# GpSimd's wait for a landing, ahead of every second head group instead of every one

## The chip, the cores and the metric

One core of one Trainium2 chip runs the whole program. The metric is the time of one execution on the device, in microseconds; a kernel's time is the median of its runs.

## What is computed

The input is a batch of two images of 64 x 64 pixels with 256 channels, float32. Three layers follow one another.

1. A deformable attention. `x` is group-normalized, multiplied by `qkv_w` and convolved depthwise (3 x 3). From the queries come, for each pixel, each of 8 head groups and each of 9 points, an offset and a mask. At each of these 72 places the keys and values of the group's 32 channels are read, bilinearly, from the four pixels around it:

```python
v00 = gather(y0i, x0i)
v01 = gather(y0i, x1i)
v10 = gather(y1i, x0i)
v11 = gather(y1i, x1i)
out = v00 * (1 - wx) * (1 - wy) + v01 * wx * (1 - wy) + v10 * (1 - wx) * wy + v11 * wx * wy
...
attn = jnp.einsum('bgpc,bgpkc->bgpk', qh, k)
attn = jax.nn.softmax(attn, axis=-1)
out = jnp.einsum('bgpk,bgpkc->bgpc', attn, v)
```

   A projection and a residual end the layer.
2. A dense attention over the 4096 pixels of an image, with 8 heads of 32, whose Q, K, V and output projections are convolutions of width 3, after a layer norm.
3. A mixture of 8 experts (256 to 1024 to 256) with a capacity, each pixel going to its best expert.

## The kernel before

**The table and the gathers.** The kernel first makes the convolved maps of image 0 (`stage_maps`) and then a table in DRAM (`stage_tables`): one row of 256 floats (1 KB) for each pixel and head group, which holds the keys and values of the four pixels around a place. A record (`sa_rec`) has, for each tile of 128 pixels, the row numbers and the weights. The work of layer 1 behind the table is the class `Sampling` (line 559). It goes over 64 tiles of 128 pixels (32 for each image); a tile has 8 head groups. For one head group of one tile, `gather` (line 655) has GpSimd issue nine indirect DMAs (line 664), one for each point, each of 128 rows of 1 KB (one row to each partition, 131,072 bytes). Together they fill one slot, `sa_slot`, of 1152 keys and as many values a partition. There are eight slots, one for each head group; so there are 512 trains of nine, 4608 gathers in all.

Ahead of a train GpSimd waits for up to three things: at head group 0 for the tile's record (`tile_in`); from tile 1 on for the slot to be free, that is for `values_made` of the same head group of the tile before; and for the landing of the train before it (`gathered` of the head group before).

**Who uses the slots.** VectorE waits for `gathered[g]` by itself, in `q_times_k` (line 710), multiplies the keys with the query, and sums in `scores` (line 716). After four head groups come `logits`, an exponential on ScalarE (line 788) and `weights`; `values` (line 762) then multiplies the values of each of the four slots by the weights, and that is what frees a slot. TensorE sums the products (line 819) and projects.

**How it is laid beside other work.** The sampling is cut into 30 pieces a tile, and VectorE, ScalarE, TensorE and SyncE do them in program order between the steps of other stages; `turn` gives each engine the pieces up to a target. GpSimd has nothing else to do in these stages: `pool` (line 670) issues, at the start of a stage, all trains that the stage's own pieces make possible, one after the other. Every stage ends with a barrier of all engines. The stages that the sampling runs beside are, by their stretches in the profile: the maps of image 1 (`stage_maps_ahead`, 517 to 1700 us); the projections and the attention of the first query block of image 0 (to 1857 and 2057); the tables of image 1 (`stage_tables_ahead`, to 2723); then projections and attention in turn: 2723 to 2880 and to 3492, to 3855 and 4905, to 5077 and 6554 (image 0), to 6684 and 6931, to 7059 and 7729, to 7857 and 8803 (image 1). A projection stage can begin only when the sampled tiles that it reads are stored. The last gather is issued at 8416 us. After 8803 come the last projection, the last attention without sampling (8892 to 9949), mixing and routing (`stage_mix_route`, which scatters rows to the experts with indirect DMAs at line 2166), and the experts.

**The dense attention's loop.** In `stage_attention` a slot is one block of 128 keys against 1024 queries. 38 slots (`TILE_SLOTS`) take one tile of sampling along. In each slot VectorE does one `a_above` (line 1654) of a bank that TensorE fills (`a_late`, line 1506), and TensorE waits for VectorE to free that one bank.

Of the kernel before, what the change touches and what calls it, by code (L numbers as in the profile page):

```python
# [17 lines left out]
G, K, HC = 8, 9, C // 8  # L18
# [540 lines left out]
class Sampling:  # L559
# [95 lines left out]
    def gather(self, pool, n, g):  # L655
        if g == 0:
            pool.wait_ge(self.tile_in[n % 2], 32 * (n // 2) + 32)
        if n > 0:
            pool.wait_ge(self.values_made, G * (n - 1) + g + 1)
        if G * n + g > 0:  # L660
            before = G * n + g - 1
            pool.wait_ge(self.gathered[before % G], 16 * K * (before // G + 1))
        for k in range(K):
            pool.indirect_dma_start(  # L664
                out=self.slot[g][:, k, :, :, :].rearrange("p c a n -> p (c a n)"), out_offset=None,
                in_=self.s["table"][n // TILES].rearrange("t p (g n) -> (t p g) n", g=G),
                in_offset=bass.IndirectOffsetOnAxis(ap=self.rec[n % 2][:, g * K + k:g * K + k + 1].bitcast(U32), axis=0),
            ).then_inc(self.gathered[g], 16)
# [2091 lines left out]
```

## Time and profile before

| | us |
|---|---|
| Median of 3 runs (10973.56 to 10993.63) | 10989.29 |
| The profiled execution | 10980.76 |
| Its span, first to last instruction | 10979.0 |
| Busy in the span: TensorE / VectorE / ScalarE / GpSimd | 7942.1 / 5184.5 / 3774.6 / 5030.1 |

The profiled execution is 8.5 us under the median, and 1.8 us of it lie outside the span. A gather's duration is the time in which GpSimd makes the descriptors of one indirect DMA; the transfer itself runs on the DMA engines behind it. "Issue" as what ended a wait means that the engine waited for nothing that the profile shows.

### The profile page before, as it was taken

What the parts mean: (1) busy time and instruction counts of PE and PEld (TensorE: products, weight loads), DVE (VectorE), ACT (ScalarE), POOL (GpSimd) and SP (SyncE); (2) the same over time, 40 slices, a digit from 0 to 9 for tenths busy, and PEclk for the clock granted to TensorE, in tenths of its full rate; (3) what the DMA queues carried; (4) which work ended last, traced back from release to release, by engine and by line L of the source; (5) the groups of instructions that cost most, each with busy time, mean ns of one, the idle gap of its engine ahead of it and who ended that gap; (6) DMA issues with size and microseconds to landing.
All of it is one profiled execution on the core that took longest, in us unless ns stands there. A gap on an engine that the chain in (4) does not pass through costs nothing. (4 is left out here: it accounts for less than half of the span.)

```text
span 10979.0 us, 96354 instructions
## 1 busy us (share of the span) xinstructions
PE 7942.1 (72%) x31522; PEld 4244.0 (39%) x31522; DVE 5184.5 (47%) x10029; ACT 3774.6 (34%) x5495; POOL 5030.1 (46%) x4864
## 2 busy tenths in 40 slices
PE   7635554642686378876888867688588979998699
PEld 3623222442343144333443433343344434444366
DVE  7432323544454355554655545455454346663233
ACT  2100001300253045442555543255255625552132
POOL 1065655555566656665665666566564000000322
PEclk9867776875898689887998888798799979998799
DMA  3824334565443344434434334443443121104221
GB/s 122 315 83 114 102 100 142 174 205 164 144 126 94 124 126 123 117 111 135 123 116 124 109 114 141 148 127 103 146 118 92 34 83 47 54 19 131 95 78 53
DMA packets 658544, 1283.57 MB, mean 117 GB/s; under 512 B 189043, under 2 KB 398218, under 8 KB 643408
## 3 DMA queue, kind: packets, MB, share of 16 engines
q0 software_dynamic: 234240, 639.57, 19.2%
q1 hardware_dynamic: 405392, 562.58, 17.2%
q10 hardware_dynamic: 18432, 75.51, 1.7%
q8 instruction: 243, 3.98, 0.2%
q14 instruction: 237, 1.94, 0.1%
HBM read 1003.44 MB, written 278.91 MB: 117 GB/s over the span
## 5 line engine op out<-in xcount | busy, mean ns | idle before, releaser
L664 POOL DMA_INDIRECT sa_slot<-s_table,sa_rec x4608 | 4773.1, 1036 | 3610.2 <-DMA sa_slot<-s_table,sa_rec 1554.8
L1654 DVE CUSTOM_DVE_ANT_0 a_above<-a_late,a_above 128x512 f32<-128x512 f32 x1600 | 1102.7, 689 | 1696.8 <-PE a_late L1506 1030.3
L1561 PE MATMUL a_ctx<-a_p,a_v 128*64 128x512 f32 x6400 | 1669.8, 645 | 102.6 <-issue 101.6
L1595 ACT ACTIVATE a_above<-a_diff 128x512 f32<-128x512 f32 x1600 | 956.5, 598 | 2270.6 <-PE a_diff L1494 1268.8
L1586 ACT ACTIVATE a_p<-a_s 128x1024 f32<-128x1024 f32 x1600 | 1629.2, 1021 | 179.8 <-PE a_s L1544 123.2
L710 DVE TENSOR_TENSOR sa_slot<-sa_slot,sa_q 128x1152 f32<-128x1152 f32 x512 | 694.1, 1356 | 1728.3 <-DMA sa_slot<-s_table,sa_rec 1710.6
L1506 PE MATMUL a_late<-a_k,a_q 96*128 96x512 f32 x1600 | 831.4, 520 | 426.0 <-DVE a_pair_max L1654 355.3
L819 PE MATMUL sa_sums<-keep_ident,sa_vals 128*128 128x128 f32 x4608 | 688.6, 299 | 589.0 <-DVE sa_vals L762 586.7
L1494 PE MATMUL a_diff<-a_kd,a_q 96*128 96x512 f32 x1600 | 745.9, 466 | 506.7 <-DMA a_q<-s_q 434.6
L1544 PE MATMUL a_s<-a_q,a_k 98*128 98x512 f32 x3200 | 1079.5, 422 | 30.8 <-ACT a_p L1586 30.6
L819 PEld LDWEIGHTS sa_sums<-keep_ident,sa_vals 128*128 128x128 f32 x4608 | 616.4, 157 | 686.3 <-DVE sa_vals L762 606.9
L1506 PEld LDWEIGHTS a_late<-a_k,a_q 96*128 96x128 f32 x1600 | 324.1, 203 | 1344.8 <-issue 824.3
L1561 PEld LDWEIGHTS a_ctx<-a_p,a_v 128*64 128x64 f32 x6400 | 422.1, 144 | 904.7 <-issue 818.2
L2161 POOL MEMSET x_ctx<- 128x2 f32 x2 | 0.2, 104 | 1532.6 <-POOLq L75 1532.6
L1982 DVE TENSOR_REDUCE a_chunk_max<-a_max 128x1 f32<-128x512 f32 x896 | 553.1, 681 | 309.2 <-PE a_max L1858 309.1
L716 DVE TENSOR_REDUCE sa_dots<-sa_slot 128x36 f32<-128x1152 f32 x512 | 691.0, 1350 | 7.0
L762 DVE TENSOR_TENSOR sa_vals<-sa_slot,sa_corner 128x1152 f32<-128x1152 f32 x512 | 681.4, 1355 | 1.8
L1544 PEld LDWEIGHTS a_s<-a_q,a_k 98*128 98x128 f32 x3200 | 602.8, 199 | 161.5 <-ACT a_p L1586 44.8
L1933 ACT ACTIVATE a_p<-a_s 128x1024 f32<-128x1024 f32 x448 | 455.0, 1024 | 452.6 <-PE a_s L1891 447.3
L1494 PEld LDWEIGHTS a_diff<-a_kd,a_q 96*128 96x128 f32 x1600 | 331.3, 207 | 642.5 <-DMA a_q<-s_q 437.0
L1160 PE MATMUL p_c<-p_hT,p_w 128*128 128x512 f32 x1152 | 520.7, 611 | 11.5 <-DMA p_wb<-in_bqkv 10.5
L1858 PE MATMUL a_max<-a_k,a_q 96*128 96x512 f32 x896 | 379.1, 477 | 64.1 <-DVE a_chunk_max L1982 40.2
(280 smaller groups left out, 8150.5 us busy)
## 6 DMA issues: line engine op xcount, KB each, us to landing
sa_slot<-s_table,sa_rec POOLq DMA_INDIRECT x4608
s_table<-t_rows ACTq DMA_DIRECT2D x64, 1024.0 KB, 7.5
a_q<-s_q SPq DMA_DIRECT2D x480, 128.0 KB, 2.5
s_part<-a_o SPq DMA_DIRECT2D x160, 256.0 KB
t_qwin<-s_dwq SPq DMA_DIRECT2D x64, 512.0 KB
t_kvwin<-s_dwkv SPq DMA_DIRECT2D x64, 386.0 KB
a_kd<-s_kd SPq DMA_DIRECT2D x384, 64.0 KB
a_o<-s_part SPq DMA_DIRECT2D x96, 256.0 KB, 2.6
```

What stands on the lines that cost most here:

```text
L664: pool.indirect_dma_start(out=self.slot[g][:, k, :, :, :].rearrange("p c a n -> p (c a n)"), out_offset=None, in_=self.s["table"][n // TIL ...
L710: t.inc(dve.tensor_tensor(k, k, q, ALU.mult))
L716: t.inc(dve.tensor_reduce(self.dots[g // 4][:, g % 4, :, :].rearrange("p k c -> p (k c)"), k, AX_X, ALU.add))
L762: dve.tensor_tensor(self.vals[:, :, j * HC:(j + 1) * HC], v, w.to_broadcast([P, 4 * K, HC]), ALU.mult)\
L819: mm = pe.matmul(self.ps_sum[i], self.vals[:, j, :], self.keep.ident[:, :], start=(j == 0), stop=(j == 4 * K - 1), is_transpose=True)
L1494: pe.matmul(self.ps_diff, self.q[run.n % self.QR][0:3 * HD, t * P:(t + 1) * P], self.kd_tile(run.head, g)[:, :], start=True, stop=True).th ...
L1506: pe.matmul(self.ps_late, self.q[run.n % self.QR][0:3 * HD, t * P:(t + 1) * P], self.k[run.head % self.KR][0:3 * HD, at:at + CHUNK], start ...
L1544: mm = pe.matmul(self.ps_s[slot % 2][:, i * CHUNK:(i + 1) * CHUNK], self.k[run.head % self.KR][:, kb * P:(kb + 1) * P], self.q[run.n % sel ...
L1561: mm = pe.matmul(self.ps_ctx[i * 2 * HD:(i + 1) * 2 * HD, :], self.v_and_ones(run.head, kb), self.p[slot % P_SLOTS][:, i * CHUNK:(i + 1) * ...
L1586: act.activation(self.p[slot % P_SLOTS][:, :], self.ps_s[slot % 2], ACT.Exp, scale=float(HD) ** -0.5).then_inc(self.exped, 1)
L1595: act.activation(self.above[slot % n][:, :], self.ps_diff, ACT.Relu).then_inc(self.diff_got, 1)
L1654: dve.tensor_tensor_reduce(above, self.ps_late, above, 1.0, LOWEST, ALU.add, ALU.max, self.pair_max[:, t, j:j + 1]).then_inc(self.late_got, 1)
```

## The change

The wait for the landing of the train before is kept ahead of head groups 0, 2, 4 and 6 of a tile and left out ahead of 1, 3, 5 and 7. The other two waits stay as they are, and so does VectorE's own wait for each slot.

```diff
         if n > 0:
             pool.wait_ge(self.values_made, G * (n - 1) + g + 1)
-        if G * n + g > 0:
+        if G * n + g > 0 and g % 2 == 0:
             before = G * n + g - 1
             pool.wait_ge(self.gathered[before % G], 16 * K * (before // G + 1))
         for k in range(K):
```

## Rows read from the trace of the kernel before

**Rows 1.** The page's groups: line engine op, names, count; busy, mean ns; idle before.

```profile
L664 POOL DMA_INDIRECT sa_slot<-s_table,sa_rec x4608 | 4773.1, 1036 | 3610.2 <-DMA sa_slot<-s_table,sa_rec 1554.8
L710 DVE TENSOR_TENSOR sa_slot<-sa_slot,sa_q 128x1152 f32<-128x1152 f32 x512 | 694.1, 1356 | 1728.3 <-DMA sa_slot<-s_table,sa_rec 1710.6
```

**Rows 2.** Line 664 alone: durations (ns), its waits and who waited (us, times).

```profile
L664 POOL DMA_INDIRECT sa_slot<-s_table,sa_rec x4608: 940/946/7615, 522.5 to 8416.3; - x192
its engine sat idle before it (us, times) until:
  DMA sa_slot<-s_table,sa_rec: 1554.8, 465
  issue: 1279.4, 4103
  DMA sa_q<-s_qpix: 524.7, 3
  POOLq L75: 148.4, 15
  DVE sa_vals L762: 102.9, 22
who waited for it (us, times):
  DVE sa_slot L710: 1710.6, 205
```

**Rows 3.** The timeline, all engines, 2163.5 to 2171: start us, us, engine line [idle before].

```profile
2164.89 0.95 POOL L664 DMA_INDIRECT sa_slot<-s_table,sa_rec  x1 [0.30 <-issue]
2167.83 1.36 DVE L710 TENSOR_TENSOR sa_slot<-sa_slot,sa_q 128x1152 f32<-128x1152 f32 x1 [11.43 <-DMA sa_slot<-s_table,sa_rec]
2168.57 1.44 POOL L664 DMA_INDIRECT sa_slot<-s_table,sa_rec  x1 [2.73 <-DMA sa_slot<-s_table,sa_rec]
...
2170.31 0.95 POOL L664 DMA_INDIRECT sa_slot<-s_table,sa_rec  x1 [0.30 <-issue]
```

**Rows 4.** Waits, maps of image 1 (517 to 1700): us in total, times, longest.

```profile
DVE sa_slot L710 <- DMA sa_slot<-s_table,sa_rec: 736.9, 74, 15.4
...
POOL sa_slot L664 <- DMA sa_slot<-s_table,sa_rec: 225.5, 74, 10.2
```

**Rows 5.** Waits, tables of image 1 (2057 to 2723).

```profile
POOL sa_slot L664 <- DMA sa_slot<-s_table,sa_rec: 141.8, 36, 8.1
```

**Rows 6.** Waits, attention 2880 to 3492.

```profile
POOL sa_slot L664 <- DMA sa_slot<-s_table,sa_rec: 122.5, 37, 9.7
...
DVE sa_slot L710 <- DMA sa_slot<-s_table,sa_rec: 11.6, 1, 11.6
```

**Rows 7.** Waits, attention 3855 to 4905.

```profile
POOL sa_slot L664 <- DMA sa_slot<-s_table,sa_rec: 222.2, 63, 11.9
...
DVE sa_slot L710 <- DMA sa_slot<-s_table,sa_rec: 121.4, 20, 11.6
```

**Rows 8.** Waits, attention 5077 to 6554.

```profile
POOL sa_slot L664 <- DMA sa_slot<-s_table,sa_rec: 288.6, 88, 11.6
...
DVE sa_slot L710 <- DMA sa_slot<-s_table,sa_rec: 178.8, 29, 11.6
```

**Rows 9.** Waits, last attention with sampling, up to its last gathers (7857 to 8420).

```profile
POOL sa_slot L664 <- DMA sa_slot<-s_table,sa_rec: 119.4, 34, 9.3
...
DVE sa_slot L710 <- DMA sa_slot<-s_table,sa_rec: 36.5, 6, 7.6
```

**Rows 10.** Waits, projection 1700 to 1857 (no row of VectorE's for a landing there).

```profile
POOL sa_slot L664 <- DMA sa_slot<-s_table,sa_rec: 29.6, 9, 5.7
```

**Rows 11.** Busy time of engines by stretch; then granted clock, DMA share, GB/s.

```profile
2057.00:2723.00 666.00, 247.49 (x1596) 232.90 (x1596) 298.50 (x529) 52.32 (x116) 381.26 (x378) 0.66 0.59 194
3855.00:4905.00 1050.00, 851.47 (x3500) 421.56 (x3500) 573.28 (x1192) 531.45 (x748) 637.61 (x612) 0.89 0.41 117
5077.00:6554.00 1477.00, 1198.12 (x4884) 588.06 (x4884) 802.11 (x1661) 737.58 (x1040) 907.79 (x873) 0.89 0.40 117
8892.00:9949.00 1057.00, 986.79 (x3936) 457.49 (x3936) 618.82 (x1126) 504.20 (x545) 0.00 (x0) 0.95 0.15 43
```

**Rows 12.** GpSimd's timeline, routing: first and last of 32 scatters without a wait.

```profile
10155.22 1.16 POOL L2166 DMA_INDIRECT s_buf<-x_h,x_to_row  x1 [204.92 <-DVE x_to_row L2368]
...
10195.51 0.97 POOL L2166 DMA_INDIRECT s_buf<-x_h,x_to_row  x1 [0.30 <-issue]
```

## The prediction

> **What bounds the kernel now.** The page's groups come first, because the change touches one line. Line 664, the gather, is GpSimd's costliest group: 4608 of them, 4773.1 us busy, and a large idle time before them that is mostly ended by the gathers' own landings; VectorE's line 710 is idle 1710.6 us for the same landings [rows 1]. So both the engine that issues and the engine that consumes wait on gathers. Which of them sets the pace? The view of line 664 alone answers that. The gathers run from 522.5 to 8416.3, some 7895 us. In that stretch GpSimd is busy 4773.1, has 1279.4 of issue gaps (0.3 us ahead of nearly every gather), and waits 1554.8 for landings, in 465 of the 512 trains. What is left is small: 148.4 at barriers and 102.9, in 22 trains, for a slot to be freed [rows 2]. (The 524.7 for the record is nearly all the wait at the very start.) GpSimd almost never waits for its consumer, and the consumer waits 205 times for it. A chain of gathers, gaps and landings therefore sets the time of everything up to 8416 us; it is not TensorE, though that is the busiest engine of the whole span.
>
> One train's end shows what a landing wait is made of. The last gather of a train is issued at 2164.89 and its descriptors are done 0.95 later, at 2165.84. VectorE, which wants that slot, starts at 2167.83, 2.0 us after; GpSimd's next gather starts at 2168.57, 2.7 us after [rows 3]. The nine gathers before took 11.3 us, yet the last one landed 2 us behind its issue: the transfers keep up, and the wait is the latency of the last gather, not a backlog.
>
> **The change, part by part.**
>
> *The waits that go.* Half of the trains lose their landing wait. Half of 465 waits is 232, and half of 1554.8 is 777 us; each is replaced by the ordinary gap of 0.3 us, 70 in all [rows 2]. On GpSimd's own line that is **707 us**, or 3.04 us a pair of trains.
>
> *What of it reaches the end.* A saving counts only where VectorE was waiting for gathers. I compare, stage by stage, half of GpSimd's waits (less 0.3 each) with VectorE's.
> - Maps and tables of image 1: 102 of saving against 737 of VectorE's waits [rows 4], and 65 in the tables stage [rows 5]. It all counts.
> - Attention 3855 to 4905: 102 against 121 [rows 7]; 5077 to 6554: 131 against 179 [rows 8]. It counts as far as TensorE allows. TensorE is busy 851 of 1050 and 1198 of 1477 us [rows 11]. In 948 and 1346 us that would be 0.90 and 0.89. The last attention, which has no sampling beside it, holds 987 of 1057, or 0.93 [rows 11]. So there is room, but little of it; I take 15 off for the two.
> - Attention 2880 to 3492: 56 of saving, while VectorE waited once, 11.6 us [rows 6]. There the attention itself is the bound and GpSimd catches up a lead that it can't carry over the barrier. I take 44 off.
> - Last attention with sampling: 54 against 36.5 [rows 9]. I take 18 off.
> - Short projection stages such as 1700 to 1857: about 13 of saving and no wait of VectorE's [rows 10]. There are a few like it, in some of which VectorE does wait a little; I take 25 off.
>
> 707 - 15 - 44 - 18 - 25 = **605 us**.
>
> *The waits that stay.* Ahead of an even head group GpSimd still waits for the train before, and no longer has drained the queue in the middle. What this does to the wait isn't in the trace. One bound: nothing, since the last gather lands 2 us behind its issue now and the odd trains will look the same [rows 3]; even a little less than nothing, where a transfer of another queue now delays a mid-pair landing that nobody will wait for. The other: the same traffic in 7% less time lifts the load of the DMA engines from some 0.41 to 0.44. In the tables stage, at a load of 0.59, a wait is 141.8/36 = 3.9 us, against 288.6/88 = 3.3 at 0.40 [rows 5, 8, 11]. At the high load for all of the 230 waits left that is 150 us; in proportion (0.03 of 0.19) it is 25. I take **25 off**, by the rows at 0.40, which are nearest.
>
> *Collisions of GpSimd and VectorE.* Gathers take 946 ns at the median and 1036 in the mean, 415 us in all over the median [rows 1, 2]. The first gather behind the landing took 1.44, and it ran beside VectorE's line 710, which the same landing had released; the next one took 0.95 [rows 3]. A denser line of gathers meets more of VectorE's work: generating takes 60% of the stretch now and would take 65%, so 415 x 0.08, some 35 us more. Against this, the joint release by one landing goes for half of the trains, where it cost 0.5 us in, say, half the cases: 232 x 0.5 x 0.5 = 58 less. I take **nothing** and keep 50 both ways. The Trainium skill (GPSIMD Engine Reference, Key points) says that GpSimd shares its SBUF interfaces with VectorE and contends with instructions that have two SBUF inputs. By that rule alone, without the joint release, the sum would lose these 35 us.
>
> *The price of a landing wait by another measure.* The row has 1554.8/465 = 3.34 us [rows 2]. The Trainium skill (DMA: Bandwidth & Descriptors, the anatomy of one DMA on GpSimd's path) fits 2.0 us plus the bytes at 436 GB/s; for 131,072 bytes that is an estimate of 2.3. By the page GpSimd's saving would be 232 x (2.3 - 0.3) = 464 us, not 707. The trace disagrees, and its number stands.
>
> **Sum:** 605 - 25 = 580 us. The profiled execution took 10980.8, so 10401; its runs' median is 8.5 higher, which gives 10409. I say **10405**.
>
> **The rivals.**
>
> *A. The attention becomes the bound.* TensorE waits for VectorE through a single bank (`a_late`); if the steps between two gather waits grow by what the waits shrink, the attention stages gain nothing. Then 102 and 65 from maps and tables remain [rows 4, 5], and some 30 from the projection that waits for stored tiles (3492 to 3855): 200 us, **10780**. For it: TensorE is at 0.81 of these stages, and the 2880 to 3492 stage already shows it [rows 6, 11]. Against: VectorE waits 121 and 179 us in the two long ones.
>
> *B. Slower: the queue fills.* Eighteen gathers, 2.4 MB, go in without a check. If the remaining wait grew with the train's length it would be 6.68 us: 232 x 3.34 = 775 lost against 707 won, some 70 us slower, **11060**. The point from which it decides is a remaining wait of 3.34 + 3.04 = 6.4 us. For it: one gather took 7.6 us and single waits reach 11.9 [rows 2, 7], so something does hold the queue at times. Against: landings follow issue by 2 us after nine gathers [rows 3], and 32 scatters in a row keep their 0.97 us to the last, with no gap over 0.30 [rows 12].
>
> *C. Another wait takes the place.* If the slots were not free, `values_made` would hold GpSimd where the landing did, and nothing would change, **10985**. Against: 22 waits of 512 for a slot [rows 2].
>
> **How the numbers follow.** The forecast has 0.80, A 0.12, B 0.05, C 0.03. The forecast's own range: at best the full 707 and 50 from collisions, 10230; at worst 580 - 125 (waits at the high load) - 50 (collisions) and a third of the attention's 233 lost, about 325 won, 10660. The range holds 0.8 if it drops a little of each end: **10260 to 10640**. A measurement of this kernel can tell about 0.2% (22 us) from no change. Faster by more than that: the forecast and A, 0.92. Within: C, 0.03. Slower: B, 0.05.
>
> **What would show it.** Line 664's landing waits should fall from 465 to about 235 and from 1554.8 to about 800 us, at a mean still near 3.4. A mean over 4 shows the load term too small, one over 6 rival B. Waits for a slot (`sa_vals`) should rise in the 2880 to 3492 stage and stay small elsewhere; some hundreds of us of them would mean A or C. VectorE's wait for landings should fall by about 600, to 1100. The last gather should be issued near 7810, not 8416. The attention stages of 1050 and 1477 should be near 955 and 1355, with TensorE at 0.9; if they keep their lengths while VectorE's gather waits vanish, it is A. The mean gather should stay within 10 ns of 1036. The forecast is wrong if the new waits or longer gathers take back over 250 us.

## The result, and the profile after

The changed kernel took **10238.52 us** (median of 4 runs, 10231.06 to 10243.08) beside 10991.46 for the kernel before (4 runs): ratio **0.9315**, 95% interval 0.9299 to 0.9332. The forecast was 10405 with a range from 10260. So the direction was right and the gain was larger, 753 us and not 584, past the range's faster end by 21 us.

That isn't the whole result. Run again on other chips, the same two kernels gave this:

| chip | kernel before | changed kernel | ratio (95%) |
|---|---|---|---|
| the measurement of the change | 10991 | 10239 | 0.9315 (0.9299 to 0.9332) |
| 7 | 10990 | 10239 | 0.9321 (0.9305 to 0.9337) |
| 1 | 10996 | 11202 | 1.0171 (1.0146 to 1.0196) |
| 13 | 11034 | 11396 | 1.0318 (1.0289 to 1.0347) |

For the first row no chip number is on record, and three of its four runs of the kernel before are those of the first profile. The kernel before can't tell the chips apart by its time; the changed one differs by 11%. Below, chips that behave like 7 are called **open** (the measurement of the change, 7 and 9), those like 1 **stalling** (1, 2 and 13). The two words name what the runs showed there; whether the chip itself is the cause is open.

First the changed kernel's profile as measured. The page's two groups, then line 664 alone, which answer to [rows 1, 2]:

```profile
L664 POOL DMA_INDIRECT sa_slot<-s_table,sa_rec x4608 | 4819.2, 1046 | 2854.5 <-issue 1335.5
L710 DVE TENSOR_TENSOR sa_slot<-sa_slot,sa_q 128x1152 f32<-128x1152 f32 x512 | 694.0, 1356 | 1359.8 <-DMA sa_slot<-s_table,sa_rec 1343.6
```

```profile
L664 POOL DMA_INDIRECT sa_slot<-s_table,sa_rec x4608: 943/949/8267, 516.0 to 7706.6; - x192
...
  issue: 1335.5, 4354
  DMA sa_slot<-s_table,sa_rec: 765.8, 223
...
  POOLq L75: 156.9, 15
  DVE sa_vals L762: 77.9, 13
...
  DVE sa_slot L710: 1343.6, 196
```

The landing waits went from 465 and 1554.8 us to 223 and 765.8, at 3.43 us each (3.34 before). The last gather is issued at 7706.6 and not 8416. GpSimd's line from first to last gather is 7190.6 us, against 7893.8. That is 703 of the 743 us between the two profiled executions (10980.76 and 10237.35).

The waits (us in total, times, longest) in the attention that answers to [rows 6] (now 2651 to 3217), then in the long ones of [rows 7, 8] (3552 to 4509, 4665 to 6015):

```profile
POOL sa_slot L664 <- DMA sa_slot<-s_table,sa_rec: 56.8, 17, 9.3
...
DVE sa_slot L710 <- DMA sa_slot<-s_table,sa_rec: 39.4, 8, 11.7
...
POOL sa_slot L664 <- DMA sa_slot<-s_table,sa_rec: 105.9, 30, 12.5
DVE sa_slot L710 <- DMA sa_slot<-s_table,sa_rec: 97.2, 20, 10.8
...
POOL sa_slot L664 <- DMA sa_slot<-s_table,sa_rec: 145.4, 42, 11.0
DVE sa_slot L710 <- DMA sa_slot<-s_table,sa_rec: 127.7, 25, 11.5
```

And the busy times by stretch that answer to [rows 11]:

```profile
1926.00:2504.00 578.00, 236.75 (x1596) 224.66 (x1596) 297.29 (x529) 51.49 (x116) 386.64 (x378) 0.68 0.67 224
3552.00:4509.00 957.00, 821.40 (x3500) 412.81 (x3500) 572.23 (x1192) 529.81 (x748) 646.23 (x612) 0.92 0.45 129
4665.00:6015.00 1350.00, 1156.01 (x4884) 574.95 (x4884) 800.97 (x1661) 737.64 (x1040) 918.12 (x873) 0.92 0.44 128
```

The first attention holds one surprise: in [rows 6] VectorE waited once for a landing, 11.6 us, and with fewer landing waits on GpSimd it waits *more*, 39.4 us. The two profiles were not of the same kind of chip, as the experiments show.

### The profile page after: what moved, and what is told of

Its sections match the earlier page's. It is cut to its first block and busy times, and to the rows that moved or that the text cites. A ratio compares the mean times of both kernels' runs of the same rounds, so it can differ in the third digit from the quotient of the medians.

```text
span 10235.6 us, 96102 instructions
## 1 busy us (share of the span) xinstructions
PE 7775.9 (76%) x31522; PEld 4185.9 (41%) x31522; DVE 5178.7 (51%) x10029; ACT 3770.1 (37%) x5495; POOL 5077.4 (50%) x4864
## 5 line engine op out<-in xcount | busy, mean ns | idle before, releaser
L664 POOL DMA_INDIRECT sa_slot<-s_table,sa_rec x4608 | 4819.2, 1046 | 2854.5 <-issue 1335.5
L1561 PE MATMUL a_ctx<-a_p,a_v 128*64 128x512 f32 x6400 | 1596.1, 620 | 91.9 <-issue 91.4
```

Source lines behind the costliest of these rows:

```text
L664: pool.indirect_dma_start(out=self.slot[g][:, k, :, :, :].rearrange("p c a n -> p (c a n)"), out_offset=None, in_=self.s["table"][n // TIL ...
L1561: mm = pe.matmul(self.ps_ctx[i * 2 * HD:(i + 1) * 2 * HD, :], self.v_and_ones(run.head, kb), self.p[slot % P_SLOTS][:, i * CHUNK:(i + 1) * ...
```

## The experiments

Each group of runs was on one chip, with the kernel before beside it.

### First group, chip 2: one stage, no waits, a pause put back

`five_tiles`, the change in the tiles of the attention 2880 to 3492 alone:

```diff
-        if G * n + g > 0:
+        if G * n + g > 0 and (g % 2 == 0 or not 19 <= n < 24):
```

> The wait for the landing is left out ahead of odd head groups in tiles 19 to 23 alone, the 40 trains of the attention stage that ran from 2880 to 3492 us. There VectorE waited for a landing once, 11.6 us, and GpSimd 122.5 us. Theory 1 (each stage ends when GpSimd has issued the stage's own trains, because all engines meet at the barrier): the stage of 612.6 us shrinks by half of GpSimd's waits less the gaps, to some 557, its last gather still 8 to 15 us ahead of its end, and the whole run is 50 to 60 us faster. Theory 2 (the step of the prediction: only VectorE's waits for landings can be saved): the stage stays over 600 us and the run gains at most 12.

`dwell`, the changed kernel with a pause ahead of the odd trains; its memsets fill a tile that nobody reads:

```diff
+        if G * n + g > 0 and g % 2 == 0:
...
+        elif g % 2:
+            for _ in range(6):
+                self.idled_n += 1
+                pool.memset(self.idle[:, :], 0.0).then_inc(self.idled, 1)
+                pool.wait_ge(self.idled, self.idled_n)
```

> The changed kernel, and ahead of every odd head group GpSimd, in place of the wait for the landing, does six small memsets in a chain, each waiting for the one before (some 3 us; the trace gives the figure). The queue is not drained, but GpSimd's time is spent all the same. Theory 1 (what counts is the length of GpSimd's line): the time goes back up by 256 times what a chain takes, so to about 10990 for 3 us, and the last gather is issued near 8416 again. Theory 3 (the wait did harm or good in another way, by what is in flight or by the clock): the time stays over 200 us away from that sum.

`no_wait`, with no landing wait at all:

```diff
-        if G * n + g > 0:
-            before = G * n + g - 1
-            pool.wait_ge(self.gathered[before % G], 16 * K * (before // G + 1))
```

> GpSimd waits for no landing at all; free slots and the tile's record alone hold it. Theory 1 with GpSimd still the bound: the 223 waits left (765.8 us) go, less 0.3 each, 698 us: 9540. Theory 1 with TensorE next: it is busy 0.86 of the long attention stages now and reaches 0.93 without sampling, so these give some 7% (270 us) and the rest gives its full share: 9750 to 9800, with VectorE's waits for landings much smaller and GpSimd waiting for sa_vals instead. Rival B (the queue fills): gathers get longer than 1.2 us in the mean or landings come over 6 us behind, and the time is over 10240.

`before_again`, the kernel before, for its profile:

> The kernel before, unchanged, for a second profile. The changed kernel was also faster in stages that the change does not touch: mixing and routing 385.0 to 363.1 us, experts 644.6 to 634.7. If this varies from one execution to the next, this profile differs from the first by as much; if it comes from the change, it repeats 385 and 645 within 3 us.

Measured beside a kernel before of 11012.74: `five_tiles` 11079.78, ratio 1.0074 (1.0056 to 1.0092), its stage 691 us long and not 612; `dwell` 10787.27, 0.9808 (0.9784 to 0.9832); `no_wait` 12304.71, **1.1169** (1.115 to 1.1189); `before_again` 11019.87. Two of these are slower where the length of GpSimd's line says faster, so a second effect exists. A stretch of `no_wait` shows it (busy us of TensorE, its weight loads, VectorE, ScalarE, GpSimd, with instructions; then clock, DMA share, GB/s):

```profile
4245.00:4255.00 10.00, 7.01 (x31) 3.23 (x29) 6.54 (x18) 5.17 (x8) 7.56 (x9) 1.00 0.36 106
4255.00:4262.00 7.00, 5.13 (x21) 3.20 (x21) 1.95 (x2) 1.06 (x2) 5.48 (x6) 0.76 0.37 105
4262.00:4268.00 6.00, 1.45 (x9) 0.85 (x7) 0.00 (x0) 0.00 (x0) 4.48 (x6) 0.78 0.35 102
4268.00:4274.00 6.00, 0.00 (x0) 0.00 (x0) 0.00 (x0) 0.00 (x0) 4.47 (x6) 0.50 0.34 102
4274.00:4280.00 6.00, 1.65 (x3) 0.83 (x3) 0.00 (x0) 1.51 (x2) 4.51 (x5) 0.50 0.38 110
4280.00:4284.00 4.00, 0.00 (x0) 0.00 (x0) 0.00 (x0) 0.00 (x0) 2.85 (x3) 0.50 0.34 100
```

GpSimd goes on at its usual pace, a gather every 1.25 us, while VectorE does nothing for 22 us and TensorE nearly nothing. The last gather starts at 4282.55; the timeline has VectorE's next step at 4288.73:

```profile
4282.55 0.95 POOL L661 DMA_INDIRECT sa_slot<-s_table,sa_rec  x1 [0.30 <-issue]
```

```profile
4288.73 0.69 DVE L1651 CUSTOM_DVE_ANT_0 a_above<-a_late,a_above 128x512 f32<-128x512 f32 x1 [27.53 <-remote]
```

"Remote" is what the profile writes where it finds no event on the core that would end the wait. The gathers themselves are no longer than before (1022 ns in the mean) and wait for no landing. So the queue doesn't fill as rival B had it; the other engines stand still while gathers are issued without a pause. As far as the trace shows, the input of VectorE's step was there: TensorE's last `a_late` before it starts at 4262.29 and takes 0.50 us. In consequence GpSimd runs into its slots: it waits 2419.0 us for `sa_vals`.

### Second group, chip 1: the changed kernel itself, and where longer trains lead

`after_again` is the changed kernel, unchanged.

> The changed kernel as it is, beside the others on one chip, because its profile shows fewer of the stalls that `before_again` and `five_tiles` show and shorter mixing and expert stages. If its gain is a property of the kernel: ratio 0.93 within its interval, mixing and routing again near 384 and the experts near 641 where the profile of the same chip has them so for the kernel before, and the change's own part, first to last gather, some 700 us shorter. If the 20 to 40 us outside the sampling belong to the kernel, mixing comes out near 363 and experts near 635 again.

`two_back` waits ahead of every train, but for the train before last:

```diff
-        if G * n + g > 0:
-            before = G * n + g - 1
+        if G * n + g > 1:
+            before = G * n + g - 2
```

> Every train waits, but for the landing of the train before last, so GpSimd never drains the queue and never runs more than 18 gathers ahead. Theory 1 (only the length of GpSimd's own line counts, a landing comes 2 us behind its issue): every such wait is met when it is reached, all 465 waits of 3.0 us net go, sampling is 1400 us shorter than before, of which the attention stages let through what TensorE has room for: 9700 to 9900. Theory 2 (gathers without a pause hold up the other engines, as in the kernel without landing waits, 12305): since the wait never makes GpSimd pause, it comes out near 12300 as well.

`every_fourth` has `g % 4 == 0` where the change has `g % 2 == 0`, so trains of 36.

> A landing wait ahead of head groups 0 and 4 alone, trains of 36. Theory 1 (line length): another 116 waits of 3.0 us go, 350 less than the changed kernel, 9890, or 10000 where the attention lets through a part. Theory 2 (trains without a pause hold up the others, by the longer the train is): it is slower than the changed kernel, between 10240 and 12305, most of the loss in the attention stages where VectorE's a_above waits for something that the profile can't name.

`pause` has eight memsets in a chain ahead of even trains, in place of the landing wait; it fills the same unread tile.

> No landing wait at all, as in the kernel that took 12305; instead, ahead of head groups 2, 4, 6 and 0, GpSimd does eight small memsets in a chain, some 3.2 us, so that it pauses where the changed kernel waits and for about as long, but without asking for a landing. If a pause is what the others need: near the changed kernel, 10200 to 10350. If the question for the landing is what matters (the queue is then known to be empty): 11500 or more. The memsets fill a tile that nobody reads.

Measured beside 10996.34: `after_again` 11202.09, `two_back` 12327.39, 1.1192 (1.1164 to 1.122), `every_fourth` 12199.21, 1.1085 (1.1068 to 1.1102), `pause` 11218.49, 1.019 (1.017 to 1.0211). Line 664 in `after_again`:

```profile
L664 POOL DMA_INDIRECT sa_slot<-s_table,sa_rec x4608: 940/946/7941, 524.4 to 8620.3; - x192
...
  issue: 1419.7, 4385
  DVE sa_vals L762: 1102.7, 70
...
  DMA sa_slot<-s_table,sa_rec: 459.8, 135
  POOLq L75: 314.0, 15
```

A remaining landing wait that the trace names is 459.8/135 = 3.41 us, as ever (135 are named, where the open chip has 223; landings are missing from this trace, see "Open" below); the time went to 1102.7 us of waits for a slot, which the consumers free late. `pause`, which never asks for a landing, costs the same as `after_again` within 0.2%: what matters on this chip is not what GpSimd waits for but that it pauses. That the length of the pause counts is argued from `dwell` (10787 on chip 2), which never ran beside the changed kernel on a stalling chip. (One of four runs of `pause` took 11625.)

### Third group, chip 7: is it the kernel or the chip?

`after_3` is the changed kernel; `dwell_2` is `dwell`; `dwell_short` has three memsets and not six.

> The changed kernel once more. It took 10238 in the measurement of the change and 11202 (ratio 1.017) in `after_again`, each within 1% of itself; the kernel before took 10991 and 10996 beside them. If the chip or the session decides: anything in one of the two places, near 10240 or near 11200, steady within 1%. If there is a third place, the kernel's time is a matter of the session in more than two ways.

> The kernel `dwell` again (a pause of 2.4 us ahead of the odd trains), now beside the changed kernel itself on one chip. `dwell` took 10787. If the stalls of `after_again` come from gathers with too little pause between them: `after_3` near 11200 and this one near 10790, so that the pause makes the kernel 400 faster. If only the length of GpSimd's line counts, this one is 550 slower than `after_3`, whatever that takes.

> As `dwell`, with three memsets in the chain and not six, a pause of some 1.2 us ahead of odd trains. Theory 2 (pause): between `dwell_2` and `after_3`, some 10900 if in proportion; a minimum below both would say that the best pause lies between 0 and 2.4 us. Theory 1 (line length): 280 below `dwell_2`, near 10510.

Beside 10990.28: `after_3` **10238.73**, `dwell_short` 10482.43, 0.9535 (0.9519 to 0.9551), `dwell_2` 10744.32, 0.9778 (0.9761 to 0.9794). The chip or the session decides between the two times, and here the length of GpSimd's line accounts for nearly all of the difference. A chain of six memsets and its gap takes 2.18 + 0.27 us where the plain gap was 0.30, so 256 of them add 550 us, and 506 were measured; three (1.07 + 0.27) add 266, and 244 were measured. What ended the waits ahead of `a_above` (line 1595 of ScalarE and 1654 of VectorE), in `after_again` and then in the changed kernel as first measured:

```profile
  PE a_late L1506: 1172.2, 694
  PE a_diff L1494: 1127.6, 760
  remote: 911.1, 163
  DMA s_kd<-p_diff_lo: 877.6, 178
  issue: 732.1, 433
```

```profile
  PE a_diff L1494: 1634.6, 1147
  PE a_late L1506: 1326.1, 903
  DVE a_pair_max L1654: 301.6, 226
  ACT a_above L1595: 108.6, 82
```

On an open chip every wait there ends with a known event, and "remote" and "issue" don't appear. On a stalling one they do, and for the kernel before, in its first profile, too:

```profile
  remote: 129.2, 43
```

### Fourth group, chip 9: the long trains and the kernel before on an open chip

> Every train waits for the landing of the train before last. `two_back` took 12327 beside an `after_again` of 11202; the chip of `after_3` (10239) has not run it. If this chip is like that of `after_3`, with no stalls at a_above that the profile calls remote, and only the line's length counts: all 465 waits go, 9700 to 9900. If gathers without a pause hold up the other engines on every chip: near 12330 again.

> Trains of 36. `every_fourth` took 12199 beside `after_again`. On a chip like that of `after_3`: 9890 to 10000 if the line's length counts alone; near 12200 if the length of a train without a pause holds up the others on every chip, between them if it does so less.

> No landing waits at all, 12305 before. As `two_back_2`: 9700 to 9900 on a chip like that of `after_3` if only the line's length counts; it and `two_back_2` within 1% of each other, since the wait for the train before last is met when it is reached.

> The kernel before, for its profile beside these three. It takes 10970 to 11036 wherever it ran. If this chip is like that of `after_3`: no stalls that the profile calls remote at a_above (43 of 129 us in [rows] of the first profile), mixing near 363 and not 385, and the attention stages a little shorter, in which case gathers must be longer or the landings later to make the same sum. If it is like that of `after_again`: the stages of the first profile again.

Beside 10969.32: `two_back_2` 9671.99, **0.8815** (0.8799 to 0.8831), `no_wait_2` 9670.08, 0.8812 (0.8798 to 0.8827), `every_fourth_2` 9878.61, 0.901 (0.8991 to 0.9028), `before_3` 10970.7. The kernels that lost 11 to 12% on chips 1 and 2 win 10 to 12% here. Line 664 of `two_back_2`:

```profile
L664 POOL DMA_INDIRECT sa_slot<-s_table,sa_rec x4608: 940/946/8267, 521.2 to 7109.2; - x192
...
  DVE sa_vals L762: 95.3, 9
  DMA sa_slot<-s_table,sa_rec: 19.5, 64
```

The price of a landing wait comes out steadily on the first two steps. `before_3` has 472 of them, the changed kernel 223, `every_fourth_2` 101, `no_wait_2` none. From 10969 to 10239 a wait is worth 2.93 us, from there to 9879 2.95, and from there to 9670 2.06. The changed kernel's time is from chip 7, the others are from chip 9, and the kernel before differs by 21 us between these two (10990 and 10969); on chip 9 alone, from the kernel before to `every_fourth_2`, it is 1091/371 = 2.94. At the last step TensorE begins to bind: in `two_back_2` it is busy 802.91 of the 887 us of the first long attention, 0.91, and VectorE waits for no landing there.

```profile
3315.00:4202.00 887.00, 802.91 (x3500) 405.33 (x3500) 571.24 (x1192) 529.85 (x748) 649.90 (x612) 0.96 0.48 139
```

`before_3` is the profile of before that belongs beside the changed kernel. Its line 664, and its waits in the stage of [rows 6] (2890 to 3510 here):

```profile
L664 POOL DMA_INDIRECT sa_slot<-s_table,sa_rec x4608: 940/946/7617, 518.7 to 8431.0; - x192
...
  DMA sa_slot<-s_table,sa_rec: 1624.7, 472
...
  DVE sa_slot L710: 2034.4, 247
```

```profile
POOL sa_slot L664 <- DMA sa_slot<-s_table,sa_rec: 126.0, 37, 9.0
...
DVE sa_slot L710 <- DMA sa_slot<-s_table,sa_rec: 93.1, 15, 11.6
```

VectorE waits 93.1 us in 15 waits there, not 11.6 in one. The 11.6 is not short for want of a record: in the first profile line 710 has no other idle time in that stage. The same 2112 matmuls of that stage in four profiles: `before_3`, the first profile of before (stalling kind), `after_3`, `after_again`:

```profile
2890.00:3510.20 620.20, 501.21 (x2112) 253.23 (x2112) 344.23 (x717) 320.43 (x454) 376.60 (x360) 0.90 0.42 121
```

```profile
2879.50:3492.10 612.60, 517.50 (x2112) 255.95 (x2112) 344.61 (x717) 320.82 (x454) 370.71 (x360) 0.90 0.42 122
```

```profile
2647.40:3211.30 563.90, 491.56 (x2112) 249.83 (x2112) 343.80 (x717) 320.05 (x454) 377.14 (x360) 0.93 0.47 133
```

```profile
2705.50:3408.90 703.40, 538.90 (x2112) 262.90 (x2112) 344.62 (x717) 321.71 (x454) 373.14 (x360) 0.84 0.37 106
```

Before the change the stage is as long on either kind (620 and 613): the reading that fits is that the stalls fall into time in which VectorE would else have waited for gathers. After it, 564 and 703. The stalls are in stretches with gathers (and perhaps in mixing, which has scatters and is 22 us longer): the last attention, without sampling, takes 1057 us in the first profile of before and in `after_again`, 1057 in `after` and 1058 in `no_wait`, a kernel whose long stages with gathers are 1.3 to 1.5 times as long as on an open chip (1234 and 949 us for the maps of image 1, 1314 and 889 for the first long attention).

How the stage ends on an open chip is in the timeline of `before_3`:

```profile
3500.02 0.95 POOL L664 DMA_INDIRECT sa_slot<-s_table,sa_rec  x1 [0.30 <-issue]
3502.91 1.36 DVE L710 TENSOR_TENSOR sa_slot<-sa_slot,sa_q 128x1152 f32<-128x1152 f32 x1 [11.38 <-DMA sa_slot<-s_table,sa_rec]
3504.30 1.35 DVE L716 TENSOR_REDUCE sa_dots<-sa_slot 128x36 f32<-128x1152 f32 x1
...
3506.70 0.68 DVE L1697 TENSOR_TENSOR a_o<-a_o,a_ctx 128x512 f32<-128x512 f32 x1
...
3507.41 0.32 SPq L1469 DMA_DIRECT2D s_part<-a_o  x1
```

The last gather lands, VectorE does the sampling pieces that it stands for, and only then comes the attention's own last step (`a_o`) and its store, because VectorE does both in one order. The barrier follows. TensorE is idle from 3501 on. The stage is as long as GpSimd's line of gathers, and on an open chip a us taken off that line came out as a us off this stage (56 us, worked out below).

### Fifth group: the stage alone once more

> The change in tiles 19 to 23 alone, the attention stage of 612 to 620 us. `five_tiles` took 67 us more than the kernel before, with the stage at 691. The profile `before_3` shows that on a chip without the stalls VectorE waits 93 us for landings in that stage, not 11.6. On such a chip: half of the stage's 126 us of landing waits, less the gaps, comes out whole, 56 us less than before, stage near 564. If the step of the prediction holds there too (the attention itself is the bound): 12 us less at most. On a chip with the stalls: 67 us more again.

> The changed kernel a fourth time, to know which kind of chip the other two ran on: near 10240, or near 11200 with some 900 us at a_above that the profile calls remote.

> No landing wait, a chain of eight memsets (some 3.2 us) ahead of even trains in its place; it took 11218 beside `after_again` with 11202. On a chip like that of `after_3` the length of GpSimd's line should decide again: within 60 us of `after_4`. Anything over 150 away would mean that the landing wait itself does more than hold GpSimd up for its length.

It ran on chip 13, a stalling one, and so left its main question untested. Beside 11034.13: `five_tiles_2` 11122.06, 1.008 (1.0061 to 1.01), stage 703 us; `after_4` 11395.73; `pause_2` 11422.55, 1.0346 (1.0316 to 1.0375). It repeats that on such chips even five tiles of longer trains cost time, and that the pause and the landing wait cost the same (0.2% apart).

## Why the prediction was right, and where it was wrong

**The line.** "A chain of gathers, gaps and landings sets the time" holds on open chips with almost nothing lost. From `before_3` (chip 9) to `after_3` (chip 7) the stretch of gathers shrinks from 7912.3 to 7177.1 us, 735, and the whole span by 738. The landing waits give 850.6 (1624.7 to 774.1); gaps take back 56.4, barriers 18.3, slots 12.1 and longer gathers 28.5 (4768.9 to 4797.4 us): 735.3. The prediction's own rule, half the waits less 0.3 us each, gives 741 from the rows of `before_3` and gave 707 from [rows 2]. Between the medians beside each other on chip 7 the gain is 752 us (10990 to 10239); the kernel before is 21 us slower there than on chip 9, so the split is good to about that much.

**The step that failed: "What of it reaches the end".** It took 102 us off: 44, 18 and 25 for stages in which VectorE hardly waited, and 15 for the little room that TensorE has in the two long attentions. The 44 went for the attention 2880 to 3492: "There the attention itself is the bound and GpSimd catches up a lead that it can't carry over the barrier", so 12 of 56 us would come. On open chips that stage fell by 56.3 us (620.2 to 563.9), the whole of it. The last attention with sampling fell by 57 (947.7 to 890.7), where 36 of 54 were kept, and a short projection by 13.8 (156.9 to 143.1), near its whole 13. Only the two long attentions lost something: they fell by 94.7 (1049.6 to 954.9) and 121.3 (1474.5 to 1353.2), where half of their 226.0 and 306.1 us of landing waits, less the gaps, is 242, so 26 went and 15 had been taken off. The reading of [rows 6] was sound for the chip that it came from: there TensorE works on to 3488.5, 11 us behind the last gather. It was the profile of the stalling kind, and by the comparison above the stalls had used up VectorE's waits. Even there the stage's last gather starts at 3476.2, 16 us before the stage's end at 3492, which the prediction didn't weigh. Without the 102 the forecast is 10303, and the range, as much lower, holds the result. Of the other 64 us, 25 are the term for the waits that stay and 28 that the line of gathers shrank by 735 us and not by 707; the rest is within the 21 us by which chips differ for the kernel before. That the sum came as near as it did is partly luck: nothing in the prediction covers a stalling chip, where it would have missed by some 800 and 990 us. The stage alone was never run on an open chip, so the 56 us rest on the two whole kernels. The range's own best end was 10230 before its ends were drawn in; it would have held the result, 10260 didn't.

**The waits that stay.** 25 us were set aside for a higher DMA load. The load did rise (0.41 to 0.45 in the attention 3855 to 4905 of [rows 11]), and a wait stayed at 3.43 us against 3.44 in `before_3` (1624.7/472). The term is zero within that; the lower bound was right.

**Collisions.** Taken as 0 within 50; 28.5 us of longer gathers came. The Trainium skill (GPSIMD Engine Reference, Key points: GpSimd's shared SBUF interfaces) states the sharing; the 35 us by its rule alone were the prediction's estimate from rows, and the trace agrees with their sign. The size isn't resolved: two profiles of the changed kernel have 4819.2 and 4797.4 us of gathers, 21.8 apart, and no run changed what VectorE does beside them. A gain from fewer joint releases, 58 by estimate, isn't seen.

**The price of a wait.** 2.93 us net, 3.2 with the gap, on open chips. The Trainium skill (DMA: Bandwidth & Descriptors, the anatomy of one DMA) gave 2.0 net by its fit, and on every step but the last the trace disagrees; the last has 2.06 because TensorE binds, which is no support for the fit. The fit comes near the middle of the transfers and not the mean wait: in `every_fourth_2` the median gather lands 3.1 us behind the start of its issue, 0.95 of that descriptor work, but single ones take up to 11.8.

**Rival A** had 0.12. It doesn't occur at trains of 18 but begins at trains without a wait (2.06 us a wait, TensorE at 0.91). **Rival B** had 0.05 and 11060. On stalling chips the change is slower by 1.7 and 3.2%, but not by B's mechanism: the remaining wait, where the trace names it, is 3.41 us and not over 6.4, and `pause`, which has none, costs the same. **Rival C** was refuted on open chips (13 waits for a slot, 76.4 us); on stalling ones hundreds of us of slot waits appear (1102.7), which we read as the consequence of stalled consumers. No case of the prediction had one kernel with two times on two chips, and the 0.05 for slower was too little.

**The 40 us outside the sampling** that the first pair of profiles shows are no gain of the change: mixing takes 385.0 us in the first profile of before, 385.1 in `after_again`, 364.5 in `before_3` and 360.6 in `after_3`. It is shorter by some 22 us on open chips, whichever the kernel. The experts' 10 us (644.6 to 634.7) are no gain either: `before_3` has 641.1 and `after_3` 641.6.

**Open.** Whether it is the chip or the session (each chip was used only once). What stops the other engines while gathers are issued. And `five_tiles` on an open chip.

The rival that stands untested is the profiler itself. Every run here comes with a span and a clock, so none shows the kernel without its records being taken, and where the stalls are, records are missing. Counted in the kept traces, the semaphore updates on open chips are 141,513 in `before_3`, 141,480 in `after_3` and 141,485 in `no_wait_2`; on stalling ones they are 92,424 in the first profile of before, 74,814 in `after_again` and 67,588 in `no_wait`, fewer the denser the gathers. In the attention of [rows 6] the first profile has 4877 where `before_3` has 10360; in the last attention, without sampling and without stalls, both have all 6563. Mixing, some 22 us longer on such chips, has 4044 and 4740. So it may be the taking of records, and not the kernel's own traffic, that stalls there, or both may follow from something third. Against the first: in the maps of image 1 `after_again` has 7056 records where `after_3` has 12675, and the stage is as long (1038 and 1039 us).

## What to carry to other kernels

Where a helper engine's own line of DMAs ends each stage, take a saving on it at nearly full value: on open chips the short attention gave all of it and the two long ones 216 of 242 us. Look at what runs between the line's last instruction and the barrier, and not only at how long the consumer waits. Before a saving is costed from one profile, see whether its waits end with "remote" or "issue": such a profile lacks records and, here, showed less of the consumer's waiting than a chip without the stalls has, and a change that removes pauses should be timed on several chips. Here removing every landing wait won 12% on chip 9 (`two_back` and `no_wait`, 9672 and 9670 us, beat both kernels there) and lost 12% on chips 1 and 2; of the versions timed on both kinds only `dwell`, with a pause of 2.4 us in place of half of the waits, was faster on both kinds (0.978 and 0.981).

## What the runs showed of the hardware that was not expected

- While GpSimd issued indirect DMAs every 1.25 us, TensorE, VectorE and ScalarE of the same core stood still at times on chips 1, 2 and 13 and not on 7 and 9; in the stretch of `no_wait` shown, VectorE for 27.5 us. As measured, with the profiler's records taken, the cost grew with the length of the train: 129 us of "remote" at `a_above` with 9 gathers, 911 with 18 and 1435.5 with no pause. What stalls them isn't shown.
- On such chips the trace also lacks a third to a half of its semaphore updates (92,424 to 67,588 of some 141,500), in the stretches with gathers.
- In the stretch of `no_wait` shown the granted clock is 0.50, TensorE's lower level of 1.2 GHz, where TensorE does nothing, behind a row in which it was busy for 1.45 of 6 us at 0.78; in the stage of the four rows above the clock is 0.93 on an open chip and 0.84 on a stalling one, for the same matmuls.
- The time of the kernel with a landing wait ahead of every train (10969 to 11034) hides the difference between chips that the changed one (10239 to 11396) shows.
